# Gate rows as a job of their own, key weights loaded in whole rows, and a tail that routes the last pair one tile at a time

## The chip, the cores and the metric
One core of a Trainium2 chip runs one program. The time is device microseconds of one execution, as the median of several runs. The engines have a queue of instructions each: PE (TensorE: matmuls and transposes), DVE (VectorE), ACT (ScalarE), POOL (GpSimd, which also issues the indirect DMAs) and SP (SyncE, which issues the plain DMAs). They wait for one another through semaphores only.

## The reference
Two layers over 2048 tokens of 256 numbers (2 batches of 1024), in float32:
```python
x = x + tanh(g_xattn[0]) * xattn(_layernorm(x), ctx_768, ln_gamma, ln_beta, Wq, Wkv, Wo, bo, mask)
    # xn = layernorm(x) * gamma + beta; q = xn @ Wq; k, v = split(context @ Wkv); 16 heads of 64, 64 keys a batch
    # softmax(where(mask, q k^T / 8, -inf)) @ v, @ Wo + bo
x = x + tanh(g_ffn[0]) * ffn(_layernorm(x), gate_w, w1, w2)
    # probs = sigmoid(xf @ gate_w.T), 16 experts; the top 2 with weights top / (sum + 1e-6)
    # slot = expert * capacity + rank of the token among the expert's tokens in token order; capacity 320
    # h = gelu(padded @ w1), out = h @ w2, gathered back, weighted and summed
```
The rank is a running count over all tokens before, so the slots of a tile follow from the counts of all earlier tiles.

## The kernel before
The work has three stages.

**Setup.** A list `JOBS` is worked off by PE, ACT and DVE together: PE fills a PSUM bank (`job` in PE's block), ACT and DVE copy it out, each its part (`job` in theirs). `ctx` transposes the context and, behind it in the same bank, the gate rows with gamma and beta (`gate_in`, which DVE first centres: `gate_centred`); `kr` multiplies the context with half of the key columns of Wkv, `q` transposes Wq, `kt` turns the key rows into a block-diagonal tile, `vr` and `vt` do the same for values, and `score` and `value` fold Wq with the keys and the values with Wo. So an attention step needs only two products. SP issues all loads in one queue in program order; each has a semaphore (`ld_wk[0]`, `ld_wk[1]` for the two halves of the key columns, `ld_wq`, `ld_x[0]` for the first two tiles of x, `ld_wv`, ...). `keep_busy(n)` is n matmuls on zeros whose results are not read. The statistics of x (`stats`, DVE) and the inverse deviations (`first_norms`, POOL, nine small operations a call) are made in three groups of tiles, `NORMS`.

**Attention steps**, `s` from -2 to 15, tile by tile. In step s, PE does in this order: `turn_probs(s-2)`, `score(s)`, `turn_x1(s-3)`, `attend(s-2)` with `router(s-3)` in its middle, and for every second step the counts of a pair of tiles. POOL splits the normalised x in a high and a low part, normalises the probabilities of tile s-1 (L496), makes the second layer norm's factors (`second_norm`, L472 to L474: `l`) and sends the rows of a pair out (`dispatch`, L464: an indirect DMA to `padded` for each tile and each of its two choices, so four for a pair). DVE picks the experts of a pair: `begin`, `find`, `choose` (ending with `both`, which PE's `counts` reads), `counts_of`, `place` (ending with `slot_row`, which the dispatch reads). ACT makes the exponentials, the copies, `gate_exp` (L629, which needs `l` and the router's logits) and the rows `z2`.

**Behind the last scores** the same work for the last tiles is written out by hand on each engine. Pairs 0 to 7 are tiles 0-1 to 14-15; PAIRS is 8, LAST is 15. Then come `keep_busy(40)`, the first transposes of fetched rows (`turn`, L1323), `keep_busy(8)`, and 16 experts of about 8.2 us each. SP fetches an expert's rows (L382) when all dispatches have landed. DVE splits the first expert weights when POOL's memset of `sent` behind the last dispatch is done. POOL adds each expert's rows into `out` with indirect DMAs (L555).

## Time and profile before

| | |
|---|---|
| median of 3 runs | 346.68 us (345.93 to 347.05) |
| the profiled execution's own time | 346.99 us |
| its span, first to last instruction | 345.2 us |
| mean granted clock of TensorE | 0.966 of full |
| busy: PE, DVE, ACT, POOL | 308.5, 248.0, 208.3, 189.2 us |
| DMA | 45.68 MB, 132 GB/s over the span |

The span and the run's time differ by 1.8 us, outside of all instructions. A busy PE is the sum of matmuls that may overlap; an engine's idle time counts only where the work behind it is waited for.

### The profile page before, as it was taken

Reading aid. Unit: us, or ns where it says so; the run is one execution under the profiler, and the core shown is the slowest. Engines: PE = TensorE matmul, PEld = TensorE weight load, DVE = VectorE, ACT = ScalarE, POOL = GpSimd, SP = SyncE. Lnnn points to the kernel's source line nnn. Section 1 sums busy time; section 2 is a strip of 40 time slices with the busy share of each in tenths; the row PEclk is TensorE's granted clock in tenths of the full one; section 3 lists DMA queues with packets and bytes.
Section 4 is the critical chain, followed back from the end, with each engine's and each line's share of the span. In section 5 each row is a group of like instructions: output and inputs, shape, how many; then the busy total and the mean of one; then the engine's idle time right before and its main releaser. Section 6 shows DMA issues by size and latency. Waiting matters only on the chain. (4 is left out here: it accounts for less than half of the span.)

```text
span 345.2 us, 6232 instructions
## 1 busy us (share of the span) xinstructions
PE 308.5 (89%) x2075; PEld 267.9 (78%) x2077; DVE 248.0 (72%) x575; ACT 208.3 (60%) x569; POOL 189.2 (55%) x233
## 2 busy tenths in 40 slices
PE   5998999799999999998758999999999999999800
PEld 1446778688889898887653599999999999999700
DVE  2389787479898898988833499888888778887300
ACT  1266788578877788877534076666666666665300
POOL 7035137645877777778754006455555555656660
PEclk9999999999999999999988999999999999999955
DMA  6999999000111111112212765988777788854340
GB/s 192 261 312 255 188 186 208 25 17 17 46 48 46 50 48 46 48 48 89 82 61 79 229 205 167 243 206 207 199 200 198 200 205 212 216 102 51 45 51 8
DMA packets 40634, 45.68 MB, mean 132 GB/s; under 512 B 5445, under 2 KB 34650, under 8 KB 40602
## 3 DMA queue, kind: packets, MB, share of 16 engines
q1 hardware_dynamic: 33138, 35.78, 37.0%
q0 software_dynamic: 7424, 9.48, 15.0%
q8 instruction: 17, 0.28, 0.3%
q14 instruction: 15, 0.12, 0.1%
q10 hardware_dynamic: 40, 0.02, 0.0%
HBM read 28.02 MB, written 17.24 MB: 131 GB/s over the span
## 5 line engine op out<-in xcount | busy, mean ns | idle before, releaser
L555 POOL DMA_INDIRECT out_dram<-wqT,diag x48 | 73.5, 1531 | 74.8 <-DMA out_dram<-wqT,diag 41.4
L1339 PE MATMUL ps_scores<-value_t,score_t 128*128 128x320 f32 x384 | 59.1, 310 | 0.0
L1339 PEld LDWEIGHTS ps_scores<-value_t,score_t 128*128 128x128 f32 x384 | 56.5, 188 | 0.4 <-DVE value_t L1056 0.3
L1246 PE MATMUL ps_out<-value_t,pT 128*128 128x256 f32 x384 | 54.3, 292 | 1.9 <-issue 1.4
L1217 PE MATMUL ps_scores<-score_t,xn 128*128 128x512 f32 x192 | 54.0, 426 | 0.0
L1246 PEld LDWEIGHTS ps_out<-value_t,pT 128*128 128x128 f32 x384 | 48.8, 193 | 2.3 <-issue 2.2
L1217 PEld LDWEIGHTS ps_scores<-score_t,xn 128*128 128x128 f32 x192 | 36.3, 189 | 6.9
L712 ACT ACTIVATE ps_scores<-ps_scores 128x640 f32<-128x640 f32 x30 | 20.6, 688 | 34.1 <-PE ps_scores L1339 34.0
L464 POOL DMA_INDIRECT padded<-z,slot_row x32 | 32.4, 1012 | 12.2 <-issue 8.3
L639 ACT ACTIVATE probs<-ps_scores,row_low 128x64 f32<-128x64 f32 x128 | 38.0, 328 | 0.5 <-DVE row_low L932 0.5
L1070 DVE CAST value_t<-ps_scores 128x640 fp32r<-128x640 f32 x30 | 24.7, 824 | 18.0 <-ACT ps_scores L712 17.8
L496 POOL TENSOR_TENSOR probs<-probs,norm 128x1024 f32<-128x1024 f32 x15 | 28.6, 1906 | 10.5 <-DVE norm L900 10.5
L1355 PE MATMUL ps_out<-score_t,value_t 128*128 128x256 f32 x240 | 31.4, 287 | 0.0
L1355 PEld LDWEIGHTS ps_out<-score_t,value_t 128*128 128x128 f32 x240 | 29.3, 191 | 0.7
L639 ACT ACTIVATION_READ_ACCUMULATOR probs<-ps_scores,row_low 128x1 f32 x128 | 28.4, 222 | 0.0
L1083 DVE TENSOR_TENSOR score_t<-raw,score_t 128x1024 fp32r<-128x1024 f32 x16 | 19.3, 1214 | 5.2 <-issue 5.2
L839 DVE TENSOR_TENSOR pT<-ps_pT,pT 128x512 fp32r<-128x512 f32 x28 | 18.5, 659 | 5.8 <-ACT pT L605 5.5
L1072 DVE TENSOR_TENSOR value_t<-ps_scores,value_t 128x512 fp32r<-128x512 f32 x30 | 20.7, 691 | 1.0
L487 POOL CAST xn<-xn_full 128x256 fp32r<-128x256 f32 x16 | 6.4, 397 | 25.1 <-ACT xn_full L653 25.0
L629 ACT ACTIVATE gexp<-ps_scores,l 128x16 f32<-128x16 f32 x16 | 4.4, 276 | 25.5 <-PE ps_scores L1233 18.7
L700 ACT ACTIVATE value_t<-ps_pT 128x640 fp32r<-128x640 f32 x16 | 11.3, 705 | 12.5 <-PE ps_pT L1323 12.3
L1194 PE MATMUL ps_pT<-ident,probs 128*128 128x128 f32 x128 | 16.6, 273 | 2.4 <-POOL probs L496 2.4
(197 smaller groups left out, 650.7 us busy)
## 6 DMA issues: line engine op xcount, KB each, us to landing
raw<-in_L_ffn_w_dram SPq DMA_DIRECT2D x16, 512.0 KB
wo_sb<-in_L_ffn_w_dram SPq DMA_DIRECT2D x16, 512.0 KB
padded<-empty SPq DMA_DIRECT2D x2, 2064.0 KB, 28.9
diag<-padded SPq DMA_DIRECT2D x16, 258.0 KB
out_dram<-x SPq DMA_DIRECT2D x16, 128.0 KB
padded<-empty SPq DMA_DIRECT2D x1, 1032.0 KB, 29.9
diag<-padded SPq DMA_DIRECT2D x16, 64.5 KB
wq_sb<-in_L_xattn_Wq_dram SPq DMA_DIRECT2D x1, 1024.0 KB, 7.5
```

The lines of the kernel that those rows point to most:

```text
L464: pool.indirect_dma_start(padded, bass.IndirectOffsetOnAxis(ap=slot_row[:, r % 2, k, q:q + 1], axis=0), z2[:, (2 * r + k) % RING, q], None ...
L496: pool.tensor_tensor(probs[:, p], probs[:, p], norm[:, p, :, None].to_broadcast([P, HEADS, KEYS]), ALU.mult).then_inc(normed, 1)
L555: pool.indirect_dma_start(out, bass.IndirectOffsetOnAxis(ap=xg[0:SLOTS[k], r, k, TOKEN:TOKEN + 1].bitcast(U32), axis=0), y[0:SLOTS[k], j, ...
L639: op = act.activation(probs[:, j, n], ps_scores[:, 1, at:at + KEYS], ACT.Exp, scale=-1.0, bias=row_low[:, n:n + 1], accum_out=row_sum[:, j ...
L712: act.activation(h_at(t, h), ps_scores[:, 2 * h:2 * h + 2, 0:CAPACITY], ACT.Gelu).then_inc(h_act, 1)
L1070: dve.tensor_copy(h_high_of(p)[:, fs], h_at(t, h)).then_inc(h_high, 1)
L1072: dve.tensor_tensor(h_low_of(p)[:, fs], h_at(t, h)[:, :, 0:n], h_high_of(p)[:, fs, 0:n].bitcast(F32), ALU.subtract)
L1083: dve.tensor_tensor(w1_hl(p, 1), raw1[:, p], w1_hl(p, 0).bitcast(F32), ALU.subtract).then_inc(w1_low, 1)
L1217: op = pe.matmul(dst, xn[:, t % 2, a, c], mv, start=False, stop=last)
L1246: op = pe.matmul(ps_attn, pT[:, a, c], mv, start=c == 0 and (a, b) == PARTS[0], stop=c == HC - 1 and (a, b) == PARTS[-1])
L1339: op = pe.matmul(ps_scores[:, f, 0:CAPACITY], w1_hl(p, a)[:, c, f * P:(f + 1) * P], x_hl(p, b)[:, c], start=c == 0 and (a, b) == PARTS[0], ...
L1355: op = pe.matmul(y_bank(e, k), (h_low_of(j) if a else h_high_of(j))[:, f, k * P:(k + 1) * P], w2_hl(e % 3, b)[:, f], start=f == 0 and (a, ...
```

## The change
Setup: the key columns of Wkv come with two DMAs of whole rows (one semaphore, waited for by both `kr` jobs) in place of four of half rows; the first two tiles of x are loaded behind the value weights and no longer ahead of them; the gate rows are a job `gate` behind the two `kr` jobs, so `ctx` no longer waits for `gate_centred`, and DVE copies `ctxT` before it centres; the three `keep_busy` matmuls behind `kr` are gone. `NORMS` has four groups: tiles 8 to 11 in step 1, tiles 12 to 15 in step 4, where 8 to 15 were made in step 2. In the last step's `attend` the router comes first and the counts a quarter later.

Behind the last scores: POOL sends the first choice of tile 10, makes `l` of tile 13, sends the three left; marks tokens, makes `l` of tile 14; sends all four of pair 6; makes `l` of tile 15; and sends pair 7 in two parts, each as soon as its own slots are there. DVE routes pair 6 wholly before it makes x1 of tile 14, and pair 7 one tile at a time. PE counts pair 7 in two parts, and has `keep_busy(5)` ahead of `attend(14)` and `keep_busy(3)` ahead of `attend(15)`.
```diff
-        JOBS += [("q", n) for n in range(HC // 2)] + [("kt", n) for n in range(2)] + [("vr", n) for n in range(2)]
+        JOBS += [("gate", 0)] + [("q", n) for n in range(HC // 2)] + [("kt", n) for n in range(2)] + [("vr", n) for n in range(2)]
...
-        NORMS = ((0, X_FIRST), (X_FIRST, TILES // 2), (TILES // 2, TILES))
+        NORMS = ((0, X_FIRST), (X_FIRST, TILES // 2), (TILES // 2, TILES - 4), (TILES - 4, TILES))
...
-            for h in range(2):
-                at = h * INNER // 2
-                sp.dma_start(wkv_a[:, at:at + INNER // 2], wkv[0:P, at:at + INNER // 2]).then_inc(ld_wk[h], 16)
-                sp.dma_start(wkv_b[:, at:at + INNER // 2], wkv[P:CTX, at:at + INNER // 2]).then_inc(ld_wk[h], 16)
+            sp.dma_start(wkv_a[:, 0:INNER], wkv[0:P, 0:INNER]).then_inc(ld_wk, 16)
+            sp.dma_start(wkv_b[:, 0:INNER], wkv[P:CTX, 0:INNER]).then_inc(ld_wk, 16)
             sp.dma_start(wq_sb[:, :, :], wq.rearrange("(c p) n -> p c n", p=P)).then_inc(ld_wq, 16)
-            sp.dma_start(x_all[:, 0:X_FIRST], x_load[:, 0:X_FIRST]).then_inc(ld_x[0], 16)
             sp.dma_start(wkv_a[:, INNER:], wkv[0:P, INNER:]).then_inc(ld_wv, 16)
             sp.dma_start(wkv_b[:, INNER:], wkv[P:CTX, INNER:]).then_inc(ld_wv, 16)
+            sp.dma_start(x_all[:, 0:X_FIRST], x_load[:, 0:X_FIRST]).then_inc(ld_x[0], 16)
             sp.dma_start(x_all[:, X_FIRST:TILES // 2], x_load[:, X_FIRST:TILES // 2]).then_inc(ld_x[1], 16)
...
-            def dispatch(r, k):
+            def dispatch(r, k, choices=(0, 1)):
 
                 pool.wait_ge(z2_ready, 2 * r + k + 1)
-                for q in range(2):
+                for q in choices:
                     pool.indirect_dma_start(padded, bass.IndirectOffsetOnAxis(ap=slot_row[:, r % 2, k, q:q + 1], axis=0),
                                             z2[:, (2 * r + k) % RING, q], None).then_inc(dispatched[r % 2], 16)
 
...
-                if s == 2:
+                if s == 1:
                     first_norms(*NORMS[2])
+                if s == 4:
+                    first_norms(*NORMS[3])
...
             mark_tokens(PAIRS - 3)
             pool.wait_ge(slots_ready, PAIRS - 2)
-            dispatch(PAIRS - 3, 0)
+            dispatch(PAIRS - 3, 0, (0,))
             second_norm(LAST - 2)
+            dispatch(PAIRS - 3, 0, (1,))
             dispatch(PAIRS - 3, 1)
-            second_norm(LAST - 1)
             mark_tokens(PAIRS - 2)
             mark_tokens(PAIRS - 1)
+            second_norm(LAST - 1)
             pool.wait_ge(slots_ready, PAIRS - 1)
             dispatch(PAIRS - 2, 0)
+            dispatch(PAIRS - 2, 1)
             second_norm(LAST)
-            dispatch(PAIRS - 2, 1)
-            pool.wait_ge(slots_ready, PAIRS)
-            dispatch(PAIRS - 1, 0)
-            dispatch(PAIRS - 1, 1)
+            for k in range(2):
+                pool.wait_ge(slots_ready, PAIRS + k)
+                dispatch(PAIRS - 1, k)
             pool.memset(sent[:, :], 0.0).then_inc(rows_sent, 1)
...
                 if kind == "ctx":
                     dve.wait_ge(out_act, 1)
-                    done.done(dve.tensor_copy(small_t[:, :], bank[:, 2 * P:2 * P + DC * EXPERTS + 2 * DC]))
                     op = dve.tensor_copy(ctxT[0:CTX - P, 1], bank[0:CTX - P, P:2 * P])
+                elif kind == "gate":
+                    dve.wait_ge(out_act, n + 1)
+                    op = dve.tensor_copy(small_t[:, EXPERTS:], bank[:, EXPERTS:DC * EXPERTS + 2 * DC])
...
             dve.memset(zeros[:, :], 0.0).then_inc(idle_ready, 1)
+            job(0, *JOBS[0])
...
-            for n in range(JOB_OF[("kt", 0)]):
+            for n in range(1, JOB_OF[("kt", 0)]):
                 job(n, *JOBS[n])
```
`begin`, `find` and `choose` take the tiles a to b of a pair now, and `choose` makes `chosen` and `both` ahead of the weights:
```diff
+            def place(r, a, b, n):
+
+                dve.wait_ge(counts_read, n)
+                link.done(dve.tensor_reduce(rank[:, a:b, :], rsel[:, a:b, :, :], AX.X, ALU.add))
                 dispatch_done(dve, r - 2)
-                dve.scalar_tensor_tensor(slot_row[:, r % 2], top_i[:, :, 0:2], float(TOKENS), rank[:, :, :], ALU.mult, ALU.add
+                dve.scalar_tensor_tensor(slot_row[:, r % 2, a:b], top_i[:, a:b, 0:2], float(TOKENS), rank[:, a:b, :], ALU.mult, ALU.add
                                          ).then_inc(slots_ready, 1)
-                link.done(dve.tensor_tensor(running[:, :], running[:, :], both[:, 1], ALU.add))
+                for k in range(a, b):
+                    link.done(dve.tensor_tensor(running[:, :], running[:, :], both[:, k], ALU.add))
+
+            def counts_of_one(k):
+
+                dve.wait_ge(counted, PAIRS + k)
+                dve.tensor_tensor(rsel[:, k], chosen[:, k], count_bank(PAIRS - 1)[:, k, None, :].to_broadcast([P, 2, EXPERTS]), ALU.mult
+                                  ).then_inc(counts_read, 1)
...
-            place(PAIRS - 3)
+            place(PAIRS - 3, 0, 2, PAIRS - 2)
...
-            begin(PAIRS - 2)
+            begin(PAIRS - 2, 0, 2)
+            find(0, 2)
+            link.sync()
+            choose(PAIRS - 2, 0, 2)
             first_residual(LAST - 1)
-            find(PAIRS - 2)
             second_stats(LAST - 1)
+            low_probs(LAST, 0)
+            counts_of(PAIRS - 2)
+            place(PAIRS - 2, 0, 2, PAIRS - 1)
+            low_probs(LAST, 1)
+
+            begin(PAIRS - 1, 0, 1)
+            first_residual(LAST)
+            find(0, 1)
+            second_stats(LAST)
             link.sync()
-            choose(PAIRS - 2)
-            low_probs(LAST, 0)
-            low_probs(LAST, 1)
-            counts_of(PAIRS - 2)
-            place(PAIRS - 2)
-
-            first_residual(LAST)
-            second_stats(LAST)
-            begin(PAIRS - 1)
-            find(PAIRS - 1)
+            choose(PAIRS - 1, 0, 1)
+            counts_of_one(0)
+            place(PAIRS - 1, 0, 1, PAIRS)
+            begin(PAIRS - 1, 1, 2)
+            find(1, 2)
             link.sync()
-            choose(PAIRS - 1)
-            counts_of(PAIRS - 1)
-            place(PAIRS - 1)
+            choose(PAIRS - 1, 1, 2)
+            counts_of_one(1)
+            place(PAIRS - 1, 1, 2, PAIRS + 1)
+
...
                     pe.wait_ge(ld_ctx, 16)
-                    pe.wait_ge(ld_gate, 48)
+                    pe.transpose(bank[:, 0:P], ctx_sb[:, 0:P], ident[:, :])
+                    op = pe.transpose(bank[0:CTX - P, P:2 * P], ctx_sb[:, P:CTX], ident[:, :])
+                elif kind == "gate":
                     pe.wait_ge(gate_centred, 1)
-                    pe.transpose(bank[:, 0:P], ctx_sb[:, 0:P], ident[:, :])
-                    pe.transpose(bank[0:CTX - P, P:2 * P], ctx_sb[:, P:CTX], ident[:, :])
...
-                        pe.wait_ge(ld_wk[a], 32)
+                        pe.wait_ge(ld_wk, 32)
...
-                if n in (0, N_ROWS - 1):
-                    keep_busy(5 if n == 0 else 3)
+                if n == 0:
+                    keep_busy(5)
...
-                    if c == HC // 2:
-                        between()
+                    if c in between:
+                        between[c]()
...
+            def count_one(k):
+
+                wait(pe, counts_read, PAIRS - 1 + k)
+                pe.wait_ge(chosen_ready, PAIRS + k)
+                to = count_bank(PAIRS - 1)
+                pe.matmul(to[:, k], ones_b[:, :], running[:, :], start=True, stop=False)
+                pe.matmul(to[:, k], before[:, :], both[:, k], start=False, stop=True).then_inc(counted, 1)
+
...
+                between = {}
+                if exists(s - 3):
+                    between[HC // 2] = lambda: router(s - 3)
+                if counted_here and r >= LATE_PAIR:
+                    between[HC - 2] = lambda: counts(r)
                 if exists(s - 2):
                     attend(s - 2, between)
...
             turn_probs(LAST - 1)
             turn_x1(LAST - 2)
-            attend(LAST - 1, lambda: router(LAST - 2))
+            keep_busy(5)
+            attend(LAST - 1, {HC // 2: lambda: router(LAST - 2)})
             turn_probs(LAST)
+            counts(PAIRS - 2)
             turn_x1(LAST - 1)
-            counts(PAIRS - 2)
-            attend(LAST, lambda: router(LAST - 1))
+            keep_busy(3)
+            attend(LAST, {HC // 2: lambda: router(LAST - 1)})
             turn_x1(LAST)
+            count_one(0)
             router(LAST)
-            counts(PAIRS - 1)
+            count_one(1)
```
PE at the program's start, before: zeros for `keep_busy`, then the context and `gate_in` transposes, two `kr` jobs of two products each, three matmuls on zeros, and Wq.
```order
L1170 MATMUL ps_misc<-zeros 128x512 x5
L1112 MATMUL ps_scores<-ident,ctx_sb 128x128
L1113 MATMUL ps_scores<-ident,ctx_sb 64x128
L1115 MATMUL ps_scores<-ident,gate_in 128x20
L1116 MATMUL ps_scores<-ident,gate_in 128x16
L1170 MATMUL ps_misc<-zeros 128x512 x5
L1126 MATMUL ps_scores<-wkv_a,ctxT 128x512
L1127 MATMUL ps_scores<-wkv_b,ctxT 128x512
L1126 MATMUL ps_scores<-wkv_a,ctxT 128x512
L1127 MATMUL ps_scores<-wkv_b,ctxT 128x512
L1170 MATMUL ps_misc<-zeros 128x512 x3
L1141 MATMUL ps_scores<-ident,wq_sb 128x128 x16
```
After:
```order
L1190 MATMUL ps_misc<-zeros 128x512 x5
L1130 MATMUL ps_scores<-ident,ctx_sb 128x128
L1131 MATMUL ps_scores<-ident,ctx_sb 64x128
L1190 MATMUL ps_misc<-zeros 128x512 x5
L1146 MATMUL ps_scores<-wkv_a,ctxT 128x512
L1147 MATMUL ps_scores<-wkv_b,ctxT 128x512
L1146 MATMUL ps_scores<-wkv_a,ctxT 128x512
L1147 MATMUL ps_scores<-wkv_b,ctxT 128x512
L1135 MATMUL ps_scores<-ident,gate_in 128x20
L1136 MATMUL ps_scores<-ident,gate_in 128x16
L1161 MATMUL ps_scores<-ident,wq_sb 128x128 x16
```
The two `gate_in` transposes moved behind the four products, and the three `keep_busy` matmuls went.

POOL in steps 1 and 2 before, from the split of tile 2 on (`ln_a` to `ln_nb` are the nine operations of `first_norms`; xn is the split, probs the normalising):
```order
L487 CAST xn<-xn_full 128x256
L488 TENSOR_TENSOR xn<-xn_full,xn 128x256
L496 TENSOR_TENSOR probs<-probs,norm 128x1024
L487 CAST xn<-xn_full 128x256
L488 TENSOR_TENSOR xn<-xn_full,xn 128x256
L440 TENSOR_SCALAR ln_a<-mv 128x8
L441 TENSOR_TENSOR ln_b<-ln_a,power 128x8
L442 TENSOR_TENSOR ln_c<-ln_b 128x8
```
After, from the same split:
```order
L485 CAST xn<-xn_full 128x256
L486 TENSOR_TENSOR xn<-xn_full,xn 128x256
L438 TENSOR_SCALAR ln_a<-mv 128x4
L439 TENSOR_TENSOR ln_b<-ln_a,power 128x4
L440 TENSOR_TENSOR ln_c<-ln_b 128x4
L441 TENSOR_TENSOR ln_a<-ln_c,mv 128x4
L442 TENSOR_SCALAR ln_c<-ln_a 128x4
L443 TENSOR_TENSOR ln_d<-ln_c,power 128x4
L444 TENSOR_TENSOR ln_r<-ln_b,ln_d 128x4
L445 TENSOR_TENSOR ln_a<-ln_r,mv 128x4
L446 TENSOR_SCALAR ln_nb<-ln_a 128x4
L494 TENSOR_TENSOR probs<-probs,norm 128x1024
```
The norms, half as wide, stand one split earlier, ahead of the normalising of tile 1; nine like them, for tiles 12 to 15, stand behind the normalising of tile 3.

POOL behind the last scores, before, from the last two dispatches of pair 5 on (l is `second_norm`; the row with two marks pairs 6 and 7):
```order
L464 DMA padded<-z,slot_row 32768x258 [waits z2_ready]
L464 DMA padded<-z,slot_row 32768x258
L472 TENSOR_TENSOR l<-mv,eps_c 128x1 [waits z2_ready,stats2_ready]
L473 TENSOR_TENSOR l<-l,power 128x1 [waits pool_done]
L474 TENSOR_SCALAR l<-mv,l 128x1 [waits pool_done]
L457 TENSOR_TENSOR z<-token,zeros 128x4 [waits dispatched1]
L457 TENSOR_TENSOR z<-token,zeros 128x4 [waits dispatched0,pool_done]
L464 DMA padded<-z,slot_row 32768x258 [waits z2_ready,slots_ready,pool_done]
L464 DMA padded<-z,slot_row 32768x258
L472 TENSOR_TENSOR l<-mv,eps_c 128x1 [waits z2_ready,stats2_ready]
L473 TENSOR_TENSOR l<-l,power 128x1 [waits pool_done]
L474 TENSOR_SCALAR l<-mv,l 128x1 [waits pool_done]
```
After, from tile 14's `second_norm` on:
```order
L470 TENSOR_TENSOR l<-mv,eps_c 128x1 [waits z2_ready,stats2_ready,pool_done]
L471 TENSOR_TENSOR l<-l,power 128x1 [waits pool_done]
L472 TENSOR_SCALAR l<-mv,l 128x1 [waits pool_done]
L462 DMA padded<-z,slot_row 32768x258 [waits z2_ready,slots_ready]
L462 DMA padded<-z,slot_row 32768x258
L462 DMA padded<-z,slot_row 32768x258 [waits z2_ready]
L462 DMA padded<-z,slot_row 32768x258
L470 TENSOR_TENSOR l<-mv,eps_c 128x1 [waits z2_ready,stats2_ready]
L471 TENSOR_TENSOR l<-l,power 128x1 [waits pool_done]
L472 TENSOR_SCALAR l<-mv,l 128x1 [waits pool_done]
L462 DMA padded<-z,slot_row 32768x258 [waits z2_ready,slots_ready]
L462 DMA padded<-z,slot_row 32768x258
```
Two dispatches of pair 6 moved from behind tile 15's `second_norm` to ahead of it, and the last pair's second half waits for slots of its own.

## Rows read from the trace of the kernel before
**Rows 1.** The page, TensorE in 40 slices of the span.
```profile
PE   5998999799999999998758999999999999999800
```

**Rows 2.** Timeline, 0 to 14 us: start, duration, engine, line, what, idle before.
```profile
1.23 2.31 PE L1170 MATMUL ps_misc<-zeros 128*128 128x512 bf16 x5 [1.23 <-DVE zeros L797]
...
3.43 0.59 SPq L336 DMA_DIRECT2D wq_sb<-in_L_xattn_Wq_dram  x1
...
5.08 0.67 SPq L339 DMA_DIRECT2D wkv_b<-in_L_xattn_Wkv_dram  x1
...
6.61 0.44 PE L1112 MATMUL ps_scores<-ident,ctx_sb 128*128 128x128 f32 x1 [3.06 <-DVE gate_in L801]
...
9.62 1.87 PE L1126 MATMUL ps_scores<-wkv_a,ctxT 128*128 128x512 f32 x2
...
11.42 1.12 PE L1127 MATMUL ps_scores<-wkv_b,ctxT 64*128 64x512 f32 x2
```

**Rows 3.** DMA issues by line, last column the us to landing.
```profile
ctx_sb<-in_ctx_dram SPq DMA_DIRECT2D x1, 96.0 KB, 2.2
...
wkv_b<-in_L_xattn_Wkv_dram SPq DMA_DIRECT2D x2, 128.0 KB, 4.1
...
wq_sb<-in_L_xattn_Wq_dram SPq DMA_DIRECT2D x1, 1024.0 KB, 7.5
...
wkv_b<-in_L_xattn_Wkv_dram SPq DMA_DIRECT2D x1, 256.0 KB, 10.4
```

**Rows 4.** Timeline, 13.5 to 40 us, from the first query transposes to the first z.
```profile
15.24 1.91 PE L1141 MATMUL ps_scores<-ident,wq_sb 128*128 128x128 f32 x16
...
18.43 0.75 DVE L784 BATCH_NORM_STATS2 stats<-x_all 128x6 f32<-128x256 f32 x2
...
24.12 0.44 PE L1298 MATMUL ps_misc<-ident,z 128*128 128x128 f32 x2
```

**Rows 5.** Timeline of POOL and PE between 53 and 78 us.
```profile
53.59 1.91 POOL L496 TENSOR_TENSOR probs<-probs,norm 128x1024 f32<-128x1024 f32 x1 [5.93 <-DVE norm L900]
...
56.73 0.25 POOL L440 TENSOR_SCALAR ln_a<-mv 128x8 f32<-128x8 f32 x1
...
62.04 0.26 POOL L448 TENSOR_SCALAR ln_nb<-ln_a 128x8 f32<-128x8 f32 x1
...
66.57 1.09 PE L1194 MATMUL ps_pT<-ident,probs 128*128 128x128 f32 x8 [2.38 <-POOL probs L496]
...
77.91 0.40 POOL L487 CAST xn<-xn_full 128x256 fp32r<-128x256 f32 x1 [4.10 <-ACT xn_full L653]
```

**Rows 6.** Timeline behind the last scores, all engines.
```profile
164.80 1.66 PE L1246 MATMUL ps_out<-value_t,pT 128*128 128x256 f32 x12 [1.44 <-issue]
...
171.47 2.67 PE L1246 MATMUL ps_out<-value_t,pT 128*128 128x256 f32 x12 [0.46 <-DVE pT L959]
...
173.40 1.06 POOL L464 DMA_INDIRECT padded<-z,slot_row  x1 [1.79 <-issue]
...
177.88 0.18 POOL L472 TENSOR_TENSOR l<-mv,eps_c 128x1 f32<-128x1 f32 x1 [2.16 <-DVE mv L977]
...
178.81 0.27 POOL L474 TENSOR_SCALAR l<-mv,l 128x1 f32<-128x1 f32 x1
...
181.56 0.22 DVE L1002 TENSOR_REDUCE both<-chosen 128x32 bf16<-128x64 bf16 x1
...
182.44 10.05 PE L1170 MATMUL ps_misc<-zeros 128*128 128x512 bf16 x39 [0.23 <-issue]
...
187.12 0.96 POOL L464 DMA_INDIRECT padded<-z,slot_row  x1 [0.30 <-issue]
...
189.63 0.38 SPq L382 DMA_DIRECT2D diag<-padded  x1
...
193.08 0.92 PE L1323 MATMUL ps_pT<-ident,diag 128*128 128x128 f32 x6 [0.59 <-DMA diag<-padded]
```

**Rows 7.** Stretch of L1170 alone: PE busy, PEld busy, granted clock, DMA.
```profile
182.00:185.00 3.00, 2.56 (x6) 1.04 (x8) 0.50 0.21 70
```

52 lines of the change are left out of this document (23 added, 29 removed).

## Prediction
> **What bounds the kernel now.** First the page's slices [rows 1]: TensorE (PE) is at 9 tenths or more almost everywhere, with four dips: the first slice (5), the eighth (7), the 19th to 22nd behind the last scores (8, 7, 5, 8), and the end. Between the dips PE is the bound, so what an earlier start saves in front of such a stretch is carried through it one for one. So I went through the places where PE waits, and asked at each what ends the wait last.
>
> The head, from its timeline [rows 2]. PE runs five matmuls on zeros to 3.54 us and then idles for 3.06 us. What ends this idle time is DVE centring the gate rows, which the context's transposes wait for although they don't read them. The first `kr` product then starts at 9.62, and the query transposes at 15.24 [rows 4]. The first `kr` pair takes 1.80 us (9.62 to 11.42), the next two matmuls of the same width 1.12: PE still ran at half pace, behind its idle stretch.
>
> The middle [rows 5]. At 66.57 PE has waited 2.38 us for POOL's normalising, because POOL made the norms of eight tiles from 56.73 to 62.30, 5.57 us in one piece. That is the page's eighth slice.
>
> The tail [rows 6], read backwards: the first transposes of fetched rows start at 193.08, when expert 0's rows land. Their DMA was issued at 189.63, 1.55 us behind the last dispatch's end at 188.08; that is the fourth dispatch of the last pair, at 1.26 us each (0.96 and 0.30 between). Beside this chain runs another, which is nearly as long: `both` of the last pair ends at 181.78, PE counts, and 40 matmuls on zeros last until 192.49. PE waits only 0.59 us for the rows behind them.
>
> **The head's terms.** The context lands 2.2 us after the queue's first issue [rows 3], no later than the first zeros end. Its two transposes then follow at about 3.5. From the first transpose to the first `kr` product it was 3.01 us (6.61 to 9.62), with four transposes and five zeros; without the two of the gate rows I take 2.7, so `kr` could start at 6.2 instead of 9.62, **3.4 us earlier**; bound 3.1. The key weights: the last of their four DMAs was issued before the queries' at 3.43 and took 4.1 us, so all had landed by 7.5 in half rows. Two whole-row DMAs carry the same bytes with two issues less; I take landing by 6.2, bound 7.5, that is a cost of 0 to 1.3.
>
> Then the pace. Before, PE reached full pace about when the second pair started. Now it has no 3 us hole, and has been busy since 1.23, so I take the first pair at full pace: 1.80 less 1.12 is **0.7 saved**; bound 0. The trace agrees with a rule of the Trainium skill, "TensorE: Matmul & The Clock Gate", section "What's actually happening": throttled is the default state, and activity releases it. By the rule alone the five zeros in front could go at full pace too, for another 1.1; by the rows alone it is 0.7, and the sum has 0.7. The three removed zeros and their gap stood between about 14.6 (11.42 and three more pairs at 1.05) and 15.24, 0.6 us; the gate transposes come back for 0.4: **0.2 saved**. The sum is 4.3, so the query transposes at 10.9. The query weights landed at 3.43 + 7.5 = 10.9: just in time.
>
> Against this stands the load that moves back. DVE takes x's first statistics at 18.43 and PE needs the z made from them at 24.12, with no slack on either [rows 4]; 4.3 earlier is 14.1. The two tiles of x now come behind the value weights, whose last part landed at 5.08 + 10.4 = 15.5. Three issues (1.65 us, as between 3.43 and 5.08) and 256 KB fewer are ahead of those weights now, which is worth 1 to 2 us; behind them x needs perhaps 0.7. I take x at 14.5, that is **0.4 lost**; bounds 0 (it lands by 14.1) and 2.1 (at 16.2, nothing gained on the queue). The value products are needed at about 13.6 and share this bound. DVE's centring now runs behind its copy of `ctxT`, to about 7, but `gate` is only asked for at 10.4; a wait there would need 3.4 us more. The copies of the job (two small ones) lie beside `kr`'s. Head: **3.9 us, from 2.2 to 4.3**.
>
> **The norms.** Taking the 5.57 us out of step 2 removes the 2.38 us wait; some 0.1 stays, since POOL's split, `l` and normalising fill the time nearly to where PE comes free. The two new calls have four tiles each. The one in step 1 begins behind the split of tile 2 and has POOL's idle 5.93 us as cover (before 53.59). The one in step 4 has the idle 4.10 us before 77.91. Nine operations on four tiles take at most 5.57; small operations here are mostly fixed cost, so I take 4.4, which overshoots the second cover by 0.3, and PE's slack behind it hides that. At 5.57 it would cost up to 1.4 once. Norms: **2.3 us, from 0.9 to 2.4**.
>
> **The tail's terms.** Three parts.
> The router ahead of the counts in the last step lets PE go on without waiting for DVE's `centred`, but the next wait (the last tile's exponentials, copies and low parts on ACT and DVE) ends when it did: nothing. POOL making `l` of tile 13 between the two dispatches takes it off that tile's gate, which is then bound by PE's router logits; DVE spends the gained 0.3 us, and more, on routing pair 6 before x1 of tile 14, so x1 and the low parts of tile 15 come about 0.5 later, and `attend(15)` starts at about 171.9 instead of 171.47. The five and three zeros stand in PE's idle time: 5 at full pace are 1.1 us (0.21 each, half of the 0.43 of the cold ones) in a hole of 1.44 (before 164.80); if cold they take 2.1, a loss of 0.7.
>
> Then POOL. Pair 6 starts at 173.40 as before, but all four dispatches now run before `l` of tile 15: 173.40 + 4 x 1.26 = 178.4. Before, POOL began this `l` at 177.88 as soon as the statistics were there (it had idled for 2.16). So POOL is what ends last now, and `l` of tile 15, 1.20 us long, is ready at 179.7 instead of 179.08: **0.6 lost**. It has a cushion: whatever pace `attend(15)` has, its statistics come by 178.5. Behind `l`, before, `both` took 2.7 us (179.08 to 181.78) for two tiles. Now it is one tile, and the weights come behind `both`: I take 2.2, so `both` at 181.9 and, with tile 14's `place` perhaps still on DVE, 182.0.
>
> From `both` on, two chains. Rows: two dispatches fewer, 188.08 - 2.52 + 0.2 = 185.8; fetch issued at 187.3; rows landed at 190.8, **2.3 earlier**. Zeros: 40 of them behind the last count, 10.7 us from `both`, as before: they end at 192.7. So the stall goes into the zeros: PE turns the first rows at 192.7, only **0.4 us earlier** than 193.08, and the zeros end 1.9 us behind the rows. DVE's splits of the expert weights start with POOL's memset 2.3 earlier and stay ahead. Tail: **0.4, from 1.5 lost to 0.6 gained**, with the zeros' pace fixed; their pace is the fourth rival.
>
> **Sum.** 3.9 + 2.3 + 0.4 = 6.6 us. The profiled execution took 346.99 (span 345.2 and 1.8 around it), so 340.4; it stood 0.3 above the median of three, 346.68, which gives **340.1**. The experts are bound by PE from the first product on, and the last adds follow them.
>
> **The rivals.**
> 1. *The loads bind the head*: x or the value weights land at 16.2. For it: their last part had the longest landing of all [rows 3], and x stood ahead before. Against it: fewer and longer rows ahead. Head 2.2, total 4.9: 341.8.
> 2. *The tail pays for its order*: POOL held by pair 6, DVE by tile 14's placing, `attend(15)` at half pace, so `both` at 183.5 to 184. That costs 1.5 to 2: 342.0. For it: POOL had 2.16 us of idle that is now used up.
> 3. *The head gains little*: the key weights in one piece arrive at 7.5 or later, PE idles again and does `kr` at half pace (1.3 + 0.7 lost), and x, behind all of them, comes at 17.5 to 18.4. What is left is the norms, the tail and at most 0.9 of the head: 343.1 to 344.0; with the tail's 1.5 and the norms' 1.4 lost as well, it is within 0.3% of no change.
> 4. *The clock holds in the tail.* From 182 to 185 PE was granted 0.50 [rows 7], and the zeros paid for it: 40 at full pace (0.21) are 8.5 us rather than 10.05. The added zeros shorten PE's idle stretches. Then the zeros end at 191.2, and `attend(15)` (12 matmuls took 2.67 us from 171.47, and 1.66 from 164.80) is quicker but hidden: 338.6. Against it: PE still has little to do from 177 to 182. The Trainium skill, in "TensorE: Matmul & The Clock Gate", section "What's actually happening", has activity release the throttle; taken strictly it speaks against this rival, for the same idle stretch.
> 5. *Slower, one mechanism*: PE stays at half pace through the 40 zeros (five took 2.31 us cold, 0.43 each, so 17.1 us, 7.1 more) and the next eight and the first products, 1.7 and more. It decides once it loses 6.6 + 1.0 us, that is if half pace lasts past the eight zeros: 348 to 349. Nothing in the rows has PE busy and cold for so long: full pace came 5 us after 6.61.
>
> **Chances.** Forecast 0.57 (its own range 339.3 to 341.2); rival 1 0.12; rival 2 0.12; rival 3 0.07, of which 0.03 within the bound; rival 4 0.08; rival 5 0.04. A measurement of this kernel tells 0.3%, 1.0 us, from no change. Faster: 0.57 + 0.12 + 0.12 + 0.08 + 0.04 = 0.93; within: 0.03; slower: 0.04. The range, 338.4 to 342.6, holds the forecast, both middling rivals and most of rival 4; it leaves out rivals 3 and 5 and the far ends.
>
> **What the profile of the changed kernel would show.** Head: the context transposes at 3.5 to 3.7, the first `kr` product at 6.2 to 6.5 with 1.1 us to the next pair, query transposes at 11, the first z transposes at 20 to 20.5 with no wait for x. Middle: no PE wait over 1 us for POOL's normalising, in step 4 or elsewhere. Tail: four dispatches back to back before the last `l`; rows landed near 2 us before the 40 zeros end, and PE's first turn right behind them without waiting. The forecast is wrong if x's statistics wait, if the norms of step 4 push the normalising late, or if the last `both` moves by more than 1 us.

## The result, and the profile after

The changed kernel is faster: its time is 0.984 of the time before, 95% interval 0.981 to 0.987. On 346.68 us that makes 341.1, against 340.1 predicted with a range of 338.4 to 342.6.

That ratio leaves the longer executions out, and for this kernel they are half of the matter. Of 20 executions eight took 339.9 to 341.0 us, one 344.2, ten 345.6 to 347.3, and one 356.0. The median of all 20 is 345.7, where the same chip gave 347.2 for the kernel before (20 executions, 344.1 to 359.8): by the medians of all, 1.5 us are gained and not 5.6. The profiled execution (346.23 us, span 344.5) is one of the long ones, so the rows of after below show what goes wrong in these; the good case is read from the experiments.

The slices of PE's busy time and clock, from the page of after, beside [rows 1]:

```profile
PE   6997999999999999999849999999999999999800
PEclk9589999999999999999996999999999999999965
```

The dip of the eighth slice is gone. A clock of 5 in the second slice is new. The head, from the timeline of PE in after:

```profile
1.23 2.31 PE L1190 MATMUL ps_misc<-zeros 128*128 128x512 bf16 x5 [1.23 <-DVE zeros L802]
3.34 0.42 PE L1130 MATMUL ps_scores<-ident,ctx_sb 128*128 128x128 f32 x1
3.76 2.22 PE L1190 MATMUL ps_misc<-zeros 128*128 128x512 bf16 x5
8.16 1.14 PE L1146 MATMUL ps_scores<-wkv_a,ctxT 128*128 128x512 f32 x2 [2.18 <-DMA wkv_b<-in_L_xattn_Wkv_dram]
9.23 2.07 PE L1147 MATMUL ps_scores<-wkv_b,ctxT 64*128 64x512 f32 x2
15.56 3.67 PE L1161 MATMUL ps_scores<-ident,wq_sb 128*128 128x128 f32 x16
```

The context's transposes no longer wait for the gate rows: 3.34 instead of 6.61 [rows 2]. But PE then waits 2.18 us for the key weights, and 1 us into `kr` two matmuls of 512 columns take 2.07 us instead of 1.12. The query transposes end at 19.2 where they ended at 17.2 before [rows 4]. The granted clock of the same stretches (start:end, length, PE busy, clock, DMA share, GB/s):

```profile
8.00:9.00 1.00, 0.84 (x2) 1.00 1.00 401
9.00:11.00 2.00, 2.00 (x3) 0.54 1.07 375
17.00:19.00 2.00, 2.00 (x11) 0.50 0.96 313
19.00:21.00 2.00, 2.00 (x12) 0.90 1.06 344
```

The four stretches of 2 us from 11 to 19 all read 0.50: the 1.2 GHz level, for 10 us in which PE was never idle. The middle, from PE's timeline in after: turns of the probabilities, beside [rows 5]:

```profile
65.99 1.05 PE L1214 MATMUL ps_pT<-ident,probs 128*128 128x128 f32 x8
82.32 1.09 PE L1214 MATMUL ps_pT<-ident,probs 128*128 128x128 f32 x8 [0.28 <-POOL probs L494]
```

No wait of 2.38 us ahead of the third turn. The tail, PE, DVE, POOL and SP's queue in after, beside [rows 6]:

```profile
171.47 1.66 PE L1266 MATMUL ps_out<-value_t,pT 128*128 128x256 f32 x12 [0.26 <-DVE pT L965]
172.50 1.06 POOL L462 DMA_INDIRECT padded<-z,slot_row  x1 [0.39 <-issue]
176.20 0.16 DVE L983 BATCH_NORM_AGGREGATE mv<-stats 128x2 f32<-128x6 f32 x1
176.39 0.96 POOL L462 DMA_INDIRECT padded<-z,slot_row  x1 [0.30 <-issue]
177.38 0.20 POOL L470 TENSOR_TENSOR l<-mv,eps_c 128x1 f32<-128x1 f32 x1
178.32 0.27 POOL L472 TENSOR_SCALAR l<-mv,l 128x1 f32<-128x1 f32 x1
180.46 0.18 DVE L1007 TENSOR_REDUCE both<-chosen 128x16 bf16<-128x32 bf16 x1
180.84 11.64 PE L1190 MATMUL ps_misc<-zeros 128*128 128x512 bf16 x40
183.22 0.96 POOL L462 DMA_INDIRECT padded<-z,slot_row  x1 [0.30 <-issue]
185.72 0.38 SPq L380 DMA_DIRECT2D diag<-padded  x1
192.32 0.86 PE L1351 MATMUL ps_pT<-ident,diag 128*128 128x128 f32 x6
```

The last scatter ends 3.9 us earlier than before (184.18, 188.08), the first fetch of rows is issued 3.9 us earlier too (185.72, 189.63), and the first turn begins 0.76 us earlier, right behind the zeros, which now take 11.64 us.

### The profile page after: what moved, and what is told of

Same layout as the page of the kernel before. It is cut to its first block and busy times, and to the rows that moved or that the text cites. A ratio compares the mean times of both kernels' runs of the same rounds, so it can differ in the third digit from the quotient of the medians.

```text
span 344.5 us, 6264 instructions
## 1 busy us (share of the span) xinstructions
PE 313.1 (91%) x2081; PEld 269.7 (78%) x2081; DVE 251.9 (73%) x585; ACT 209.1 (61%) x570; POOL 191.8 (56%) x242
## 5 line engine op out<-in xcount | busy, mean ns | idle before, releaser
L1266 PE MATMUL ps_out<-value_t,pT 128*128 128x256 f32 x384 | 53.4, 289 | 0.6 <-DVE pT L965 0.6
L1266 PEld LDWEIGHTS ps_out<-value_t,pT 128*128 128x128 f32 x384 | 47.7, 189 | 1.7 <-issue 1.6
L462 POOL DMA_INDIRECT padded<-z,slot_row x32 | 33.4, 1044 | 10.0 <-issue 7.1
L494 POOL TENSOR_TENSOR probs<-probs,norm 128x1024 f32<-128x1024 f32 x15 | 28.6, 1909 | 6.2 <-DVE norm L906 6.2
L1190 PE MATMUL ps_misc<-zeros 128*128 128x512 bf16 x66 | 20.1, 467 | 1.2 <-DVE zeros L802 1.2
L1076 DVE TENSOR_TENSOR value_t<-ps_pT,value_t 128x640 fp32r<-128x640 f32 x16 | 13.0, 814 | 8.5 <-ACT value_t L703 8.5
```

The costliest lines, as they stand in the source:

```text
L462: pool.indirect_dma_start(padded, bass.IndirectOffsetOnAxis(ap=slot_row[:, r % 2, k, q:q + 1], axis=0), z2[:, (2 * r + k) % RING, q], None ...
L494: pool.tensor_tensor(probs[:, p], probs[:, p], norm[:, p, :, None].to_broadcast([P, HEADS, KEYS]), ALU.mult).then_inc(normed, 1)
L1190: pe.matmul(ps_misc[:, :], idle_rows[:, 0:P], idle_rows, start=True, stop=True)
L1266: op = pe.matmul(ps_attn, pT[:, a, c], mv, start=c == 0 and (a, b) == PARTS[0], stop=c == HC - 1 and (a, b) == PARTS[-1])
```

## The experiments

Twelve kernels, four at a time on one chip beside the kernel before. Times are medians of all executions. A ratio is to the kernel before, run beside them on the same chip, and is taken as in the section on the result.

### Is it the wait for the key weights?

Four kernels change only what stands between the context's transposes and `kr`.

```
zeros10:         if n == 0: keep_busy(10)          (5 in after)
zeros1:          if n == 0: keep_busy(1)
half_rows:       key weights in four half-row DMAs, ld_wk[0], ld_wk[1], as before
zeros1_5behind:  keep_busy(1 if n == 0 else 5), for n in (0, N_ROWS - 1)
```

> The second block of zeros is 10 instead of 5, nothing else. In the profile of after the five zeros end at 5.98 us, TensorE then waits 2.18 us for the key weights, and the granted clock is 0.50 from 9.2 to 19 us. Theory A (the head's gain hangs on TensorE's pace behind that wait): five more zeros of 0.44 us fill the hole, `kr`, gate and query transposes run at full pace, q ends some 4 to 5 us earlier than in the profiled run, and every execution comes in at about 340 to 341 us. Theory B (the two groups of times of after, 340 to 341 and 345.7 to 347, come from something elsewhere): the times still fall into both groups. Theory C (the head is bound by loads behind the key weights, x and wq): the clock is held but the time stays within 0.5 us of the lower group at best.

> The second block of zeros is 1 instead of 5, so TensorE idles some 4 us ahead of `kr` instead of 2.18 us. Theory A (TensorE's pace behind the wait): the clock falls in every execution, the pairs of `kr` take 2.07 us each, and all times are in the upper group, 345.5 to 347.5 us. Theory B (the groups have another source): still a share of times at 340 to 341.

> Key weights in half rows with two semaphores as before, all else of after kept. Before, the first half had landed by 6.1 us (issue 1.7 + 4.4) and the second about 4 us later. If whole rows are what delays `kr` (it began at 8.16 us in the profiled run against 6.2 predicted), the first pair of `kr` begins at 6.0 to 6.3 us, full pace, and then waits for the second half until about 8.5 to 10; if that second wait keeps TensorE busy enough the time is 340 to 341 throughout; if the wait only moves behind the first pair (rival: the loads move together, 1.05 MB has to land anyway) the times are as after's, both groups.

> One zero instead of five ahead of `kr`, as in the run with one zero, and five zeros behind the pairs of `kr` (2.2 us at half pace). There TensorE was busy without a pause with float32 work from 7.4 us, yet every pair, the gate and the query transposes ran at half pace until about 19.5 us, while the bfloat16 zeros from 1.2 us on had brought full pace by about 5.6 us. If bfloat16 zeros bring the pace back and float32 work does not (theory D), the query transposes that follow take 1.9 us instead of 3.7 and the time is 346.2 plus 2.2 or less for the zeros less 2 to 3 for the pace: about 345.5 to 346.5. If the pace comes back at a time of its own (rival), query transposes take 3.7 us again and the time is 348.0 to 348.5.

| | median, all executions | how many | ratio |
|---|---|---|---|
| zeros10 | 340.42 (339.56 to 341.60) | 6 | 0.983 (0.977 to 0.989) |
| zeros1 | 346.16 (345.05 to 348.39) | 12 | 1.000 (0.996 to 1.004) |
| half_rows | 340.54 (339.38 to 341.13) | 6 | 0.982 (0.976 to 0.988) |
| zeros1_5behind | 347.31 (346.17 to 348.47) | 10 | 0.999 (0.996 to 1.001) |

Theory A holds: with the hole shortened, or with the first half of the weights landing earlier, every execution is in the lower group; with the hole widened, every one is in the upper. The half rows are the cleaner of the two comparisons, since they keep the five zeros. One zero also leaves less work ahead of the hole, so that run alone doesn't tell a longer wait from a TensorE that had not reached full pace before it. Timeline of PE with ten zeros:

```profile
3.77 3.00 PE L1190 MATMUL ps_misc<-zeros 128*128 128x512 bf16 x10
7.94 1.12 PE L1146 MATMUL ps_scores<-wkv_a,ctxT 128*128 128x512 f32 x2 [1.18 <-DMA wkv_b<-in_L_xattn_Wkv_dram]
12.38 1.97 PE L1161 MATMUL ps_scores<-ident,wq_sb 128*128 128x128 f32 x16
```

The ten take 3.00 us, not twice 2.22: full pace came in the middle of them. So they fill only one of the 2.18 us that I meant them to fill, and a wait of 1.18 us is left; but this one leaves the pace alone, and so does one of 1.73 us in the run with 28 zeros. With half rows there is no wait:

```profile
3.77 2.33 PE L1192 MATMUL ps_misc<-zeros 128*128 128x512 bf16 x5
5.90 1.13 PE L1148 MATMUL ps_scores<-wkv_a,ctxT 128*128 128x512 f32 x2
8.01 1.13 PE L1148 MATMUL ps_scores<-wkv_a,ctxT 128*128 128x512 f32 x2
11.20 1.94 PE L1163 MATMUL ps_scores<-ident,wq_sb 128*128 128x128 f32 x16 [0.78 <-DVE small_t L762]
```

`kr` starts at 5.90, 2.0 us before that of ten zeros, and the first turn of the probabilities comes 0.9 earlier (44.69, 45.57). The second half was there when it was asked for at 8.01; the rival of the half rows is out. In the landings of the profile the last of its four loads came at 7.3 us (issued at 2.92, 4.4 to landing), the whole rows at 8.1 in after, 7.9 with ten zeros and 7.1 with x first (issued at 1.70; 6.4, 6.2 and 5.4 to landing). This run doesn't separate the split itself from what it puts behind the key weights: the query weights are issued at 3.43 instead of 2.30. The medians are equal all the same; "Where the tail's gain goes" says where the 0.9 us go.

With one zero, `kr` in the timeline of PE and two rows of its granted clock:

```profile
7.38 2.08 PE L1146 MATMUL ps_scores<-wkv_a,ctxT 128*128 128x512 f32 x2 [2.98 <-DMA wkv_b<-in_L_xattn_Wkv_dram]
13.39 2.07 PE L1147 MATMUL ps_scores<-wkv_b,ctxT 64*128 64x512 f32 x2
```

```profile
11.00:13.00 2.00, 2.00 (x3) 1.00 1.06 229
17.00:19.00 2.00, 2.00 (x12) 1.00 1.04 367
```

Half pace from start to end, while the record of the clock says 1.00. The durations decide here. Five zeros behind `kr`:

```profile
15.95 2.31 PE L1190 MATMUL ps_misc<-zeros 128*128 128x512 bf16 x5
18.52 2.46 PE L1161 MATMUL ps_scores<-ident,wq_sb 128*128 128x128 f32 x16
20.81 1.04 PE L1154 MATMUL ps_scores<-ident,probs 128*128 128x128 f32 x8
```

The zeros run at half pace (2.31), and full pace comes inside the query transposes, by their duration at about 19.6; in after and with one zero it came at 19 to 19.4. So theory D falls: these zeros brought nothing back, whatever did. The time, between both expectations, tells nothing by itself.

### Each part alone, and undone

```
norms_of_before      after, but NORMS in three groups, the last in step 2
norms_of_before_z10  the same, with keep_busy(10) behind the context
tail_of_before       ten zeros; all behind the last scores as before
head_only_z10        before, with the head of after and ten zeros
norms_only           before, with NORMS in four groups, steps 1 and 4
tail_only            before, with the tail of after
```

> The last two groups of first norms are one group of eight in step 2 again, as before; all else of after kept. The traces give 2.5 us gained in steps 2 and 3 and 0.4 to 0.5 lost in step 4, so this kernel should be 2.1 us slower than after (predicted for this term: 2.3, range 0.9 to 2.4): about 342.8 us where after is at 340.7, and 347.8 where after is at 345.7. Rival: the slack shows up later and the split is worth under 1 us.

> Ten zeros in the second block, and the first norms of tiles 8 to 15 in one group of eight in step 2, as before. With the head's clock held in every execution this sizes the term of the norms alone: predicted 2.3 us (0.9 to 2.4), read from the two traces 2.1 (2.5 gained, 0.4 lost in step 4), and the lower times of the same edit without the ten zeros (343.65 to 344.2) suggest 3.2. Expected 342.5 by the traces, 343.7 by those times.

> Head and norms of after with ten zeros in the second block, but everything behind the last scores as in the kernel before (the last pair routed as a pair, pauses and order as they were). Beside ten zeros with the new tail (340.4 us median). From the traces: in the profile of after the last scatters end 3.9 us earlier, but the first turn begins only 0.65 us earlier than before once the 0.11 us that it came in earlier are taken off, because the 40 zeros now end last. So this kernel should be 0.6 us slower, about 341.0 us. Rival: in the clock of a good execution the forty zeros take 10.3 us instead of 11.6, and the tail is worth up to 2 us: 342.4.

> The kernel before with the head alone changed (gate rows in a job of their own, key weights in whole rows, the order of the loads) and ten zeros in the second block, so that the clock holds there; norms and tail as before. Predicted for the head: 3.9 us (2.2 to 4.3). From the shift of the turns of the probabilities with ten zeros: 2.7 us at the first turn. If terms add, 2.7 us faster than before. Rival: in the run with the norms of before and ten zeros the wait ahead of the third turn (2.39 us) was followed by 1.5 us at half pace; if that comes in most executions the head alone brings only 1.2 us.

> The kernel before with the first norms of tiles 8 to 15 in two groups of four, steps 1 and 4; all else as before. Predicted 2.3 us faster (0.9 to 2.4), by the shift of the turns 2.1 in this profile. Rival: as the wait of 2.38 us is followed by half pace in a part of the executions, taking it away is worth up to 3.5 on the median.

> The kernel before with only what stands behind the last scores changed (scatters without pauses, last pair tile by tile, zeros there). Predicted 0.4 us faster (-1.5 to +0.6); undoing it in the version with ten zeros cost 1.4 us on two medians, and 1.97 us at the first turn of the experts in the two traces, with the clock held; in the profile of after, where the clock fell among the 40 zeros, 0.64. Expected 1.4 to 2.0 us faster. Rival: the old head leaves less to gain and it is under 0.7.

| | median, all executions | how many | ratio |
|---|---|---|---|
| norms_of_before | 346.89 (343.65 to 349.59) | 12 | 0.997 (0.993 to 1.002) |
| norms_of_before_z10 | 344.65 (343.32 to 354.51) | 6 | 0.989 (0.985 to 0.993) |
| tail_of_before | 342.47 (340.28 to 350.02) | 6 | 0.982 (0.977 to 0.986) |
| head_only_z10 | 343.05 (342.65 to 344.37) | 6 | 0.989 (0.985 to 0.994) |
| norms_only | 343.58 (342.71 to 344.41) | 6 | 0.990 (0.985 to 0.995) |
| tail_only | 345.83 (343.48 to 347.93) | 12 | 0.994 (0.989 to 0.998) |

The norms of before without the ten zeros came in both groups: three executions at 343.7 to 344.2, nine at 346.1 and over; 342.8 and 347.8 were expected. With ten zeros, the lowest is 343.3, nearer to the 343.7 that the times had suggested. Each part alone is faster than before, the norms and the head by about 1%, the tail by 0.6%. Together that is 2.7%, where all three make 1.7% (zeros10). They don't add in the times, and with an interval of half a per cent (1.6 us) on each I can't say by how much. That a pace which one part holds can't be held again by the next would explain it, and isn't shown. So the traces size them. The starts of the same work on PE (turns of the probabilities, then the first of the experts) against the kernel before, in us:

| | first turn | third | sixth | sixteenth | first turn of experts |
|---|---|---|---|---|---|
| before (start) | 48.27 | 66.57 | 90.34 | 168.18 | 193.08 |
| after | +1.95 | -0.58 | -0.12 | -0.14 | -0.76 |
| zeros10 | -2.70 | -5.24 | -4.82 | -4.80 | -6.78 |
| tail_of_before | -2.71 | -5.24 | -4.84 | -5.08 | -4.81 |
| norms_of_before_z10 | -2.82 | -2.80 | -1.29 | -1.34 | -3.10 |
| half_rows | -3.58 | -6.12 | -5.71 | -4.88 | -6.41 |
| head_only_z10 | -3.10 | -3.08 | -3.08 | -3.26 | -2.93 |
| norms_only | -1.07 | -3.62 | -3.15 | -3.12 | -4.48 |
| tail_only | -1.50 | -1.48 | +0.01 | +0.00 | -1.77 |

Read with ten zeros: the head brings 2.70, the norms 2.54 less 0.42 that step 4 takes back, so 2.1, and the tail 1.98. As 341.0 us was expected for the tail undone and 342.5 measured, that run went the way of its rival.

The last two rows carry a warning. Both kernels have the head of before, unchanged, and yet their first turn comes 1.07 and 1.50 us earlier than in the trace of before. The gate rows landed earlier there and their centring was quicker (0.34 instead of 1.14 us), so PE waited 1.15 and 1.18 us for it instead of 3.06. From PE's timeline in norms_only:

```profile
4.70 0.44 PE L1114 MATMUL ps_scores<-ident,ctx_sb 128*128 128x128 f32 x1 [1.15 <-DVE gate_in L803]
```

So the 2.70 of the head holds against one execution of before, in which the gate rows came late; against these two it is 1.6 and 1.2. In tail_only that lead is gone again by the sixth turn, through a loss of pace that the kernel before escaped.

A part undone costs more than its wait, because PE's pace may fall behind the wait. In the run with the norms of before and ten zeros (PE's timeline, and the clock of the stretch):

```profile
63.77 1.97 PE L1212 MATMUL ps_pT<-ident,probs 128*128 128x128 f32 x8 [2.39 <-POOL probs L494]
65.61 2.40 PE L1235 MATMUL ps_scores<-score_t,xn 128*128 128x512 f32 x6
```

```profile
63.00:66.00 3.00, 2.23 (x10) 0.60 0.16 56
```

The same wait in the kernel before was followed by a turn of 1.09 us [rows 5]. Here half pace behind the 2.39 us of wait cost 1.5 us more: the fourth turn follows the third by 9.45 us instead of 7.91. The trace of tail_only shows the same (9.40):

```profile
65.09 1.97 PE L1209 MATMUL ps_pT<-ident,probs 128*128 128x128 f32 x8 [2.39 <-POOL probs L496]
```

And in the run with the tail of before:

```profile
166.62 2.14 PE L1251 MATMUL ps_out<-value_t,pT 128*128 128x256 f32 x12 [0.46 <-DVE pT L964]
169.27 2.44 PE L1251 MATMUL ps_out<-value_t,pT 128*128 128x256 f32 x12
188.27 0.92 PE L1328 MATMUL ps_pT<-ident,diag 128*128 128x128 f32 x6 [0.28 <-DMA diag<-padded]
```

`attend(15)` (the last tile) is slowed as it was before (2.67 at 171.47 [rows 6]), against 1.66 and 1.67 with the new tail in after. In the traced run with the new norms alone it took 1.68 with the old tail:

```profile
168.33 1.68 PE L1248 MATMUL ps_out<-value_t,pT 128*128 128x256 f32 x12 [0.46 <-DVE pT L961]
188.60 0.93 PE L1325 MATMUL ps_pT<-ident,diag 128*128 128x128 f32 x6 [0.89 <-DMA diag<-padded]
```

That sizes the two halves of the tail's gain. From the 14th turn of the probabilities to the first turn of the experts it is 39.5 to 39.7 us in the three traces of the old tail with a slowed `attend(15)`, 38.2 in this one, and 37.6 with ten zeros and the new tail. So of the 2.0 us only 0.6 is gained on an old tail that holds its pace; 1.4 is the pace, lost in three of four traces of the old tail and in none of ten of the new one. Nor is the new tail always quick: its nine traces with 40 zeros take 37.6 to 39.0, in good part by the zeros, which take 10.3 to 11.7 us. I didn't separate the zeros ahead of `attend(15)` from the order.

### Where the tail's gain goes

```
tail28:       keep_busy(10) in the head, keep_busy(28) instead of 40 in the tail
z10_x_first:  keep_busy(10) in the head, x_all[0:2] loaded ahead of the value weights
```

> Ten zeros in the second block and 28 instead of 40 zeros ahead of the first turn of the experts. With ten zeros the 40 end at 186.3 us in the trace and the next work starts there without waiting for the rows; the second fetch is issued at 181.7, and before the rows landed 3.45 us behind that issue, which gives 185.2. If the zeros bound, the first turn comes 1.1 us earlier and the time is 339.3 us. Rivals: the raw weights or the first products bind next and nothing is gained (340.4); or TensorE idles 2 us behind the shorter block and its clock falls in the experts, several us slower (343 or more).

> Ten zeros in the second block and the load of the first two tiles of x ahead of the value weights again, as before. The prediction put 0.4 us of loss on moving it back. With ten zeros the statistics of x begin at 15.78 us right behind the copies of the query transposes, without a wait, so the load should not be what binds: within 0.3 us of ten zeros (340.4). If it is late in other executions: up to 0.4 us faster. Rival: the value weights come later and the value rows at 15.2 us wait: 0.3 to 0.8 slower.

28 zeros: 340.44 (339.89 to 340.72, 5 executions), ratio 0.978 (0.974 to 0.981). x first: 341.38 (340.59 to 344.36, 6), ratio 0.986 (0.980 to 0.992). The 339.3 expected for 28 zeros didn't come, and what took its place is neither of the rivals named. The zeros in the timeline of PE with 40:

```profile
176.21 10.26 PE L1190 MATMUL ps_misc<-zeros 128*128 128x512 bf16 x39
186.30 0.86 PE L1351 MATMUL ps_pT<-ident,diag 128*128 128x128 f32 x6
```

and with 28:

```profile
176.30 8.88 PE L1190 MATMUL ps_misc<-zeros 128*128 128x512 bf16 x28
185.02 0.86 PE L1351 MATMUL ps_pT<-ident,diag 128*128 128x128 f32 x6
```

The turn comes 1.28 us earlier, and every turn of the experts after it does, to 302.31 against 303.59. At the end nothing is left: spans of 338.6 and 338.3. The scatters into `out` on POOL with 28 zeros:

```profile
296.32 1.42 POOL L556 DMA_INDIRECT out_dram<-wqT,diag  x1 [0.30 <-issue]
301.29 1.56 POOL L556 DMA_INDIRECT out_dram<-wqT,diag  x1 [3.55 <-DMA out_dram<-wqT,diag]
328.49 1.42 POOL L556 DMA_INDIRECT out_dram<-wqT,diag  x1 [0.30 <-issue]
```

and with 40:

```profile
297.57 1.43 POOL L556 DMA_INDIRECT out_dram<-wqT,diag  x1 [0.30 <-issue]
301.46 1.56 POOL L556 DMA_INDIRECT out_dram<-wqT,diag  x1 [2.46 <-DMA out_dram<-wqT,diag]
328.09 1.43 POOL L556 DMA_INDIRECT out_dram<-wqT,diag  x1 [0.30 <-issue]
```

An expert's three scatters wait until those of the expert before have landed. The 16 first scatters follow each other at 7.5 to 9.8 us, with a mean of 8.1 with 40 zeros and 8.2 with 28, against PE's 8.2; over the last experts PE needs less (308.3 to 319.5 for one first and two second products and PE's last work), so this chain ends the kernel, at a pace set by how the landings fall: from 301.46 and from 301.29 the four last groups take 28.1 and 28.6 us. Neither the zeros bound this kernel nor PE alone. Both rivals of that run (the raw weights, the clock) are out: PE waits for nothing there, at 2.02 and 2.03 us for the first twelve products. PE's last matmul ends at 318.3 us with 28 zeros and 319.5 with 40; POOL's last scatter ends at 329.9 and 329.5.

The half rows lose their 0.9 us earlier, between the sixth turn (-5.71) and the sixteenth (-4.88), nearly all in one step: the 15th turn follows the 14th by 8.74 us instead of 7.89. PE waits 0.67 us there ahead of a router; why it does so in this trace stays open. And x first: at 44.93 its first turn is 0.64 us before that of ten zeros, but `kr` started 0.67 earlier (7.27, 7.94), as the weights had landed by 7.1. So the place of x cost nothing measurable, neither gained nor lost: the interval allows 2 us on either side, the trace 0.1.

## Why the prediction was right, and where not

**The time** was right to 1 us for the executions in which the pace holds: 339.9 to 341.0 against 340.1. That it was is in good part luck: steps that were wrong lie in it, and their errors cancel. For the other half of the executions, 345.6 us and more, only rival 3 had a place.

**Head, 3.9 (2.2 to 4.3).** Measured 2.7 with ten zeros against the trace of before (1.2 to 1.6 against the two other traces with the old head), -1.95 in the profiled execution of after. The first two steps held: the context's transposes at 3.34 (3.5 was said), no wait for the gate rows. The step that failed is "I take landing by 6.2, bound 7.5": `kr` started at 8.16 in after behind a wait for them, and at 7.3 to 8.1 in the other kernels with whole rows. Before, the key weights came in four DMAs of which the first two had landed by about 5.8 (the second issued at 1.7, 4.1 to landing [rows 3]), and the first product needs only these. With one semaphore on everything it waits for the last byte, which landed at 7.1 to 8.1 us, not at 6.2. That was a wait taken on, and I priced it as bytes with fewer issues. The load of x was sized rightly: it landed at 14.5 with ten zeros (issued at 4.07, 10.4 to landing), as said, and bound nothing, since DVE came to it only at 15.78.

**Rival 3 (0.07)** was this very case, and it came in about half of the executions. Its chance was too low, and its price too: it took half pace for `kr` alone and a late x, 343.1 to 344.0. The pace stayed at half through the gate and query transposes too, to 19 us. What they cost: the first z transposes 1.9 us later than before, where the forecast had them 3.9 earlier. x was not late: in after its statistics began at 19.99, where the copies left DVE free. "Now it has no 3 us hole" was right of the first hole and blind to the second. Nor did the slow first pair of before need a hole of 3 us: behind a wait of 1.15 us it ran at half pace too (1.91 us at 7.72 in norms_only). The Trainium skill, "TensorE: Matmul & The Clock Gate", section "What's actually happening", says that the window in which a monitor watches TensorE's activity runs freely and isn't reset when a kernel starts, and that the same kernel therefore measures differently from run to run. Twenty times the same program with two outcomes agrees with that, but no run here shows the monitor itself, and a second source isn't excluded: the whole rows landed at 7.1 to 8.1 us in different traces, so the wait itself differs between executions.

**Norms, 2.3 (0.9 to 2.4).** Measured 2.1 in the trace, by the mechanism named. A call of four tiles took 4.3 us (4.4 was said): two of its nine operations, the powers, went from 1.67 to 1.04 us and the other seven stayed as they were. Step 4 took back 0.42 where I had hidden 0.3 behind slack that PE did not have (0.28 of wait ahead of 82.32). What was missing is the pace: where PE waits 2.4 us, full pace may be lost on top (in two of five traces), so undoing the split cost 3.5 us in the trace with ten zeros (sixteenth turn), and in the times between 2.2 (by the two ratios) and 4.2 (by the two medians, of different chips).

**Tail, 0.4 (-1.5 to +0.6).** Mis-sized, the bound named rightly. The zeros did become what ends last (192.3; 192.7 was said), and PE turned the rows without a wait. POOL was also what ended last ahead of the last `l`, as said: the statistics were there at 176.36, and `l` began at 177.38, right behind the fourth dispatch of pair 6. What failed is "Pair 6 starts at 173.40 as before" and the 1.26 us for each dispatch. DVE had the pair's slots ready at 171.96 instead of 172.64, its dispatches began at 172.50, and the four took 4.85 us instead of 5.04. So `l` was ready at 178.59, 0.5 earlier than before instead of 0.6 later, and `both` at 180.64 instead of 182.0. The last scatter ended at 184.2, not 185.8. Of these 1.6 us the profiled run kept little, since 40 zeros took 11.64 us instead of 10.05; with 10.26 in zeros10 the tail brought 2.0.

The second thing missed is the pace in the old tail. `attend(15)` keeps full pace in the new one (1.66, not 2.67); I had written that this is hidden. In the new order it nearly is: POOL would have kept `l` waiting to 177.38 anyway, where the statistics came at 177.79 before. But the old tail, against which the term is measured, pays 1.4 us for it. Against an old tail that holds its pace the gain is 0.6 (norms_only), close to the 0.4 of the forecast.

**"The last adds follow them"** failed as a statement on the end, as the run with 28 zeros shows. It cost the sum nothing visible: the terms of zeros10 (2.7, 2.1, 2.0) make 6.8, the spans differ by 6.9. (These are shifts of one set of traces against one trace of before, so that they add up says little of each.)

So the sum of 6.6 was right because the head was 1.2 too large and the tail 1.6 too small, measured against the one trace of before. That is chance and not skill.

## What to carry to other kernels

Where two transfers are joined under one semaphore, price the later wait of the first consumer, not the issues saved. An idle stretch of TensorE of 2 us or more had, in a part of the executions here, a second price, its pace behind it: look at the spread of the times, and fill the hole or split the load until the spread is gone. Trace the kernel before more than once before a term is sized against it: here its head alone differed by 1.5 us between traces. And before a gain is carried "one for one" to the end, find the slowest chain of the last stage: here POOL's scatters, one expert behind the other.

## What the runs showed of the hardware

- Within the first 8 us, a wait of 3 to 3.5 us was followed by half pace in 22 of 22 executions, one of 2.2 in 11 of 20, one of 2.3 in 9 of 12 (norms_of_before), one of 1.7 or less in 0 of 17 (zeros10, half_rows, tail28). The pace is judged by the times here, and the wait is known of the traced execution of each kernel alone. A wait of 2.4 us in mid-kernel did it in two traces (norms_of_before_z10, tail_only) and not in three (before, head_only_z10, norms_of_before: the fourth turn follows the third by 7.84 to 7.91 us).
- Half pace in the head then lasted 10 to 12 us under an unbroken row of matmuls, to 19 to 19.6 us in three kernels and to about 18.7 in a fourth (norms_of_before), whether it began at 7.4 or 9.2. In mid-kernel it lasted 3 to 4 us (norms_of_before_z10, tail_only). What ends it stays open.
- The record of the granted clock read 1.00 over 12 us in which pairs of matmuls took 2.07 instead of 1.12, in two traces (zeros1, zeros1_5behind). In the profiled execution of after it read 0.50 for the same durations.
- The same DVE operation (centring 16 rows of 256, L801 of the kernel before) took 1.14 us in the trace of before and 0.34 in norms_only and tail_only; no run isolates why.
- One indirect DMA took POOL 2.04 us to issue (at 165.13 in after) where the others took 0.96 to 1.06; no run isolates why.
